# A gated delta-rule block with a routed feed-forward: the first block's solve moved into PSUM, and the head's copies, constants and loads reordered

## The reference

```python
q, k, v = x @ Wq.T, x @ Wk.T, x @ Wv.T;  gate = x @ Wg.T;  beta = sigmoid(x @ Wb.T)
alpha = exp(-exp(A_log) * softplus(x @ Wa.T + dt_bias))
q = q / norm(q) / sqrt(8);  k = k / norm(k)
def step(S, inp):                       # S: 8 x 8 for each sequence and head
    S = S * a_t
    delta = (v_t - k_t @ S) * beta_t
    S = S + outer(k_t, delta)
    return S, q_t @ S
ctx = rmsnorm(ys) * silu(gate);  x = layernorm(x + ctx @ Wo.T + bo)
# then a router picks one of 8 experts for each token: silu(x @ g.T) * (x @ u.T) @ d.T
# x = layernorm(x + that)
```

## Time and profile before

| | us |
|---|---|
| median of 3 runs | 792.31 (787.78 to 793.07) |
| the profiled execution, time | 794.0 |
| the profiled execution, span | 792.2 |
| busy: TensorE, VectorE, GpSimd, ScalarE | 682.4, 617.4, 654.0, 416.0 |
| first chunk of the recurrence starts | 39.5 |

### The profile page before, as it was taken

The page is one execution under the profiler, slowest core; times in us unless marked ns, Lnnn a source line. Parts: engine busy times, 40 slices in busy tenths (PEclk is TensorE's granted clock), DMA queues, the critical chain, the costliest instruction groups (busy, mean ns, idle before and its releaser), DMA issues.

```text
span 792.2 us, 13701 instructions
## 1 busy us (share of the span) xinstructions
PE 682.4 (86%) x3545; PEld 512.9 (65%) x3545; DVE 617.4 (78%) x1553; ACT 416.0 (53%) x1282; POOL 654.0 (83%) x799
## 2 busy tenths in 40 slices
PE   8577889999899998999989899697688869999990
PEld 3344546657576575755657566475577869999990
DVE  2699999999999999999999999999972533334340
ACT  4725454565655556564575645424224346666660
POOL 1669899989999999999999999999755765766664
PEclk9779999999999999999999999889859999999995
DMA  5922343323344233334333333204544556766730
GB/s 131 221 69 57 86 113 111 84 81 88 95 113 120 85 86 97 106 103 109 84 99 82 103 107 84 84 4 155 204 156 130 202 187 204 248 230 231 242 107 11
DMA packets 135917, 97.27 MB, mean 123 GB/s; under 512 B 95630, under 2 KB 110225, under 8 KB 135714
## 3 DMA queue, kind: packets, MB, share of 16 engines
q1 hardware_dynamic: 130514, 87.55, 37.5%
q0 software_dynamic: 4320, 8.43, 3.3%
q10 hardware_dynamic: 1008, 0.43, 0.2%
HBM read 39.80 MB, written 31.43 MB: 90 GB/s over the span
## 4 chain that ended last, share of the span: by engine, by line
DVE 36%; PE 34%; POOL 16%; issue 5%; ACT 3%; SPq 2%; DMA 1%; POOLq 0%; DVEq 0%; ACTq 0%
PE banks L432 10%; PE banks L654 8%; DVE banks L1811 6%; DVE upd L1799 6%; PE banks L445 5%; DVE banks L1785 5%; DVE prod L1769 4%; POOL q_prod L1257 4%; DVE banks L1795 4%; DVE mix L1789 3%; DVE upd L1780 3%; POOL u L1257 2%; PE banks L639 2%; PE banks L707 2%; POOL kkqk L1257 1%
## 5 line engine op out<-in xcount | busy, mean ns | idle before, releaser
L1257 POOL TENSOR_TENSOR q_prod<-s_keep,q_gam 128x512 f32<-128x512 f32 x128 | 139.9, 1096 | 17.4 <-ACT s_keep L964 16.2
L707 PE MATMUL banks<-q_prod,ident 128*128 128x256 f32 x496 | 119.1, 395 | 21.1 <-POOL q_prod L1257 21.1
L964 ACT ACTIVATE s_keep<-banks 128x128 f32<-128x128 f32 x128 | 49.7, 389 | 164.8 <-DVE upd L1799 164.8
L707 PEld LDWEIGHTS banks<-q_prod,ident 128*128 128x128 f32 x496 | 95.8, 198 | 45.8 <-POOL q_prod L1257 32.1
L542 DVE TENSOR_TENSOR hid<-banks,silu 128x384 f32<-128x384 f32 x71 | 39.6, 558 | 96.1 <-PE banks L432 85.5
L432 PE MATMUL banks<-xs_t,w_tile 128*128 128x128 f32 x852 | 108.9, 279 | 3.7 <-ACT silu L473 3.7
L1811 DVE TENSOR_REDUCE banks<-upd 128x128 f32<-128x640 f32 x127 | 105.1, 828 | 7.2
L654 PE MATMUL banks<-kkqk,ident 128*128 128x320 f32 (+2 forms) x272 | 91.5, 502 | 20.6 <-POOL kkqk L1257 8.1
L432 PEld LDWEIGHTS banks<-xs_t,w_tile 128*128 128x128 f32 x852 | 102.4, 195 | 4.6 <-issue 4.5
L1785 DVE TENSOR_REDUCE banks<-prod 128x64 f32<-128x576 f32 x128 | 93.7, 732 | 0.0
L654 PEld LDWEIGHTS banks<-kkqk,ident 128*128 128x128 f32 x272 | 60.0, 234 | 47.8 <-issue 20.7
(11 more groups left out here) (214 smaller groups left out, 1448.8 us busy)
## 6 DMA issues: line engine op xcount, KB each, us to landing
w_tile<-gate_up_we SPq DMA_DIRECT2D x71, 352.0 KB
xs<-x_sorted SPq DMA_DIRECT2D x71, 64.5 KB, 2.2
x_ct<-in_x_ct SPq DMA_DIRECT2D x16, 256.0 KB, 3.0
k_dram<-kq_s SPq DMA_DIRECT2D x16, 256.0 KB, 2.9
q_dram<-kq_s SPq DMA_DIRECT2D x16, 256.0 KB, 3.6
out<-v_s SPq DMA_DIRECT2D x16, 256.0 KB, 2.6
k_h<-k_dram SPq DMA_DIRECT2D x16, 256.0 KB, 3.1
out<-beta SPq DMA_DIRECT2D x16, 256.0 KB, 2.6
```

The lines of the kernel that those rows point to most:

```text
L707: i = mm(out, ident[:, :], q_prod[m][:, :, d, :], start=(m == 0 and d == 0), stop=(d == DH - 1), skip_group_check=True)
L1257: b.step(label, win, lambda: tt(out, x, y, op))
```

## The change

Four things, all in the head but two waits:

- Constants: dt_bias and A_log have a semaphore of their own, `s_head`, and are issued behind x_ct of block 1; z of block 0 waits for six loads. ScalarE's exp of A_log moves behind kq_s(0).
- Projections: block 0 in the order q, b, g, v; block 1 in the order k, b, g, z, q, v. The copy v_s(0) moves from ScalarE to VectorE, in front of `fold_weights`; k_n(1) moves from VectorE to GpSimd, between k_gam(0) and k_end(0). On ScalarE kq_s(1) moves behind decay_of(0), and softplus(0) ahead of k_ln(1).
- The solve of block 0: kkd, u1, u2, u3 are written to PSUM (banks of `y_ps`, after silu(1)), u1 a second time to SBUF ("u1_s"), so that each product has one operand in PSUM and one in SBUF; u_tmp and solve stay in SBUF.
- The sync queue: b_store(0) ahead of k_load(0), the loads of block 0 ahead of z_store(1), x_load of windows 2 and 3 later, the latter last.

```diff
-        n_early, n_const = 16 * 8, 16 * (len(tiles) - 7 + 2)
+        n_early, n_const = 16 * 6, 16 * (len(tiles) - 7 + 2)
...
                 load(e, s_early, "w_a", "w_q", "w_v")
+                e.dma_start(x_ct[1][:, :], t["x_ct"][:, 1, :]).then_inc(s_xct[1], 16)
                 for tile, src in ((dt_h, t["dt_bias"]), (neg_a, t["A_log"])):
                     e.dma_start(tile[:, :], src.rearrange("(h o) -> h o", o=1).unsqueeze(0)
-                                .to_broadcast([NB // 2, H, 1])).then_inc(s_early, 16)
-                e.dma_start(x_ct[1][:, :], t["x_ct"][:, 1, :]).then_inc(s_xct[1], 16)
+                                .to_broadcast([NB // 2, H, 1])).then_inc(s_head, 16)
...
                 project("q", 0, q_at, 0)
-                project("v", 2, v_at, 0)
                 project("b", 4, b_at, 0)
                 project("g", 3, g_at, 0)
+                project("v", 2, v_at, 0)
                 b.wait_dma(s_xct[1], 1)
-                b.wait(act, "z_s", 0)
-                project_heads("z", z_at, 1)
                 b.wait(dve, "k_n", 0)
                 project("k", 1, k_at, 1)
-                b.wait(act, "kq_s", 0)
-                project("q", 0, q_at, 1)
                 b.wait(act, "tanh", 0)
                 project("b", 4, b_at, 1)
                 b.wait(act, "silu", 0)
                 project("g", 3, g_at, 1)
-                b.wait(act, "v_s", 0)
+                b.wait(act, "z_s", 0)
+                project_heads("z", z_at, 1)
+                b.wait(act, "kq_s", 0)
+                project("q", 0, q_at, 1)
+                b.wait(dve, "v_s", 0)
                 project("v", 2, v_at, 1)
...
                 b.wait(act, "k_ln", a - 1)
+                b.wait(act, "kq_s", a - 1)
                 project("b", 4, pre_ps[:, 0, :])
...
                 b.step("kq_s", 0, lambda: A(kq_s[:, 1, :], pb[6], ACT.Copy))
-                b.wait(pe, "v", 0)
-                b.step("v_s", 0, lambda: A(v_s[:, :], post_ps, ACT.Copy, scale=-1.0))
-                if not b.dry:
+                if not b.dry:
+                    b.eng.wait_ge(s_head, 32)
+                    A(neg_a[:, :], neg_a[:, :], ACT.Exp).then_inc(s_neg_a, 1)
                     nc.scalar.preload_act_table_set("silu_and_others")
...
-                b.wait(pool if a > 2 else dve, "k_n", a - 1)
+                b.wait(pool, "k_n", a - 1)
...
+                b.wait(act, "k_r", 1)
+                b.wait(act, "kq_s", 1)
+                mul("k_n", 1, kq_s[:, 0, :], kq_s[:, 0, :], k_sq[:, :])
                 mul("k_end", 0, k_end[0][:, :, :, :, :].rearrange("p c b d j -> p b d j c"),
...
+                b.wait(pe, "v", 0)
+                b.step("v_s", 0, lambda: v.tensor_scalar(v_s[:, :], post_ps, -1.0, None, ALU.mult))
                 if not b.dry:
                     fold_weights(b.eng)
...
+                b.wait(act, "silu", 1)
+                kkd_ps, u1_ps = y_ps[1][:, 0:96], y_ps[1][:, 96:480].rearrange("p (n j c) -> p n j c", j=3, c=NCH)
+                u2_ps = y_ps[0][:, 0:256].rearrange("p (n j c) -> p n j c", j=2, c=NCH)
+                u3_ps = y_ps[0][:, 256:384].rearrange("p (n j c) -> p n j c", j=1, c=NCH)
...
-                for d, u in ((1, u1), (2, u2), (3, u3)):
+                for label, d, u in (("u1", 1, u1_ps), ("u1_s", 1, u1), ("u2", 2, u2_ps), ("u3", 3, u3_ps)):
...
+                b.wait(dve, "u2", 0)
+                mul("u_far", u_tmp[:, :, 0, :], u2_ps[:, :, 1, :], u1[:, :, 0, :])
+                mul("solve1", sv[:, :, 4:16:5, :], u1_ps[:, :, :, :], bh[:, :, 0:3, :])
+                b.wait(dve, "u_far", 0)
                 b.wait(dve, "u3", 0)
-                mul("solve1", sv[:, :, 4:16:5, :], u1[:, :, :, :], bh[:, :, 0:3, :])
-                mul("u_far", u_tmp[:, :, 0, :], u2[:, :, 1, :], u1[:, :, 0, :])
-                b.wait(dve, "u_far", 0)
-                mul("u3_a", u3[:, :, 0, :], u3[:, :, 0, :], u_tmp[:, :, 0, :], ALU.subtract)
+                mul("u3_a", u3_ps[:, :, 0, :], u3_ps[:, :, 0, :], u_tmp[:, :, 0, :], ALU.subtract)
                 b.wait(dve, "u3_a", 0)
-                mul("u_near", u_tmp[:, :, :, :], u1[:, :, 1:3, :], u1[:, :, 0:2, :])
+                mul("u_near", u_tmp[:, :, :, :], u1_ps[:, :, 1:3, :], u1[:, :, 0:2, :])
...
-                v_store(0, act)
-                b.wait(pe, "g", 0)
-                x_load(2)
+                v_store(0, dve)
+                b_store(0)
                 k_load(0)
-                b_store(0)
-                z_store(1, dve)
                 q_load(0)
                 v_load(0)
                 b_load(0)
+                z_store(1, dve)
                 v_store(1, dve)
-                b.wait(pe, "g", 1)
-                x_load(3)
+                x_load(2)
+                z_load(1)
                 q_store(1)
-                k_store(1, dve)
-                z_load(1)
                 v_load(1)
+                b_store(1)
+                k_store(1, pool)
                 q_load(1)
-                b_store(1)
                 k_load(1)
                 b_load(1)
+                x_load(3)
```

More of the change, by code:

```diff
@@ L171, in block_kernel @@
         s_const, s_setup, s_neg_a = sem("s_const"), sem("s_setup"), sem("s_neg_a")
-        s_wk, s_early, s_zero = sem("s_wk"), sem("s_early"), sem("s_zero")
+        s_wk, s_early, s_zero, s_head = sem("s_wk"), sem("s_early"), sem("s_zero"), sem("s_head")
         s_xct = [sem(f"s_xct{n}") for n in range(2)]
@@ L1108, in start_up @@
                 b.step("silu", 1, lambda: A(gate[1][:, :], y_ps[1], ACT.Silu))
[L1109 to L1112, removed]
                 if not b.dry:
@@ L1117, in start_up @@
                     nc.scalar.mul(neg_a[:, :], neg_a[:, :], -1.0).then_inc(s_neg_a, 1)
+                softplus(0)
                 b.wait(pe, "nk", 1)
@@ L1121, in start_up @@
                 b.step("k_r", 1, lambda: A(k_sq[:, :], k_sq[:, :], ACT.Exp, scale=-0.5))
-                softplus(0)
                 if not b.dry:
@@ L1125, in start_up @@
                 decay_of(0)
+                b.wait(pe, "q", 1)
+                b.wait_dma(s_kst, 1)
+                b.wait_dma(s_qst, 1)
+                b.step("kq_s", 1, lambda: A(kq_s[:, :, :], pre_ps[:, 0:2, :], ACT.Copy))
                 b.wait(act, "tanh", 1)
@@ L1572, in start_up @@
                     at += 2 * size
-                b.wait(act, "k_r", 1)
-                b.step("k_n", 1, lambda: v.tensor_tensor(kq_s[:, 0, :], kq_s[:, 0, :], k_sq[:, :], ALU.mult))
                 b.wait(act, "alpha", 0)
@@ L1577, in start_up @@
                 b.wait(pe, "kk", 0)
+                b.wait(act, "silu", 1)
+                kkd_ps, u1_ps = y_ps[1][:, 0:96], y_ps[1][:, 96:480].rearrange("p (n j c) -> p n j c", j=3, c=NCH)
+                u2_ps = y_ps[0][:, 0:256].rearrange("p (n j c) -> p n j c", j=2, c=NCH)
+                u3_ps = y_ps[0][:, 256:384].rearrange("p (n j c) -> p n j c", j=1, c=NCH)
                 for d in range(1, C):
-                    mul(f"kkd{d}", lag(kkd, lag_at[d], d), lag(chain_ps[0][:, 256:352], lag_at[d], d),
+                    mul(f"kkd{d}", lag(kkd_ps, lag_at[d], d), lag(chain_ps[0][:, 256:352], lag_at[d], d),
@@ L1580, in start_up @@
                         (a_h[0][:, :, 1:4, :], decays[0][:, :, 4:7:2, :], decays[0][:, :, 5:6, :])[d - 1])
                 b.wait_dma(s_bld, 1)
-                for d, u in ((1, u1), (2, u2), (3, u3)):
+                for label, d, u in (("u1", 1, u1_ps), ("u1_s", 1, u1), ("u2", 2, u2_ps), ("u3", 3, u3_ps)):
                     size = (C - d) * NCH
                     b.wait(dve, f"kkd{d}", 0)
-                    mul(f"u{d}", u[:, :, :, :].rearrange("p (e b) j c -> p e b (j c)", b=2),
+                    mul(label, u[:, :, :, :].rearrange("p (e b) j c -> p e b (j c)", b=2),
@@ L1586, in start_up @@
                         bh[:, :, d:C, :].rearrange("p (e b) j c -> p e b (j c)", b=2),
-                        kkd[:, lag_at[d]:lag_at[d] + 2 * size].rearrange("p (b n) -> p b n", b=2).unsqueeze(1)
+                        kkd_ps[:, lag_at[d]:lag_at[d] + 2 * size].rearrange("p (b n) -> p b n", b=2).unsqueeze(1)
                         .to_broadcast([P, DH, 2, size]))
+                b.wait(dve, "u2", 0)
+                mul("u_far", u_tmp[:, :, 0, :], u2_ps[:, :, 1, :], u1[:, :, 0, :])
+                mul("solve1", sv[:, :, 4:16:5, :], u1_ps[:, :, :, :], bh[:, :, 0:3, :])
@@ L1596, in start_up @@
                 b.wait(dve, "u_near", 0)
-                mul("u2_a", u2[:, :, :, :], u2[:, :, :, :], u_tmp[:, :, :, :], ALU.subtract)
+                mul("u2_a", u2_ps[:, :, :, :], u2_ps[:, :, :, :], u_tmp[:, :, :, :], ALU.subtract)
                 b.wait(dve, "u2_a", 0)
-                mul("u_last", u_tmp[:, :, 0, :], u1[:, :, 2, :], u2[:, :, 0, :])
-                mul("solve2", sv[:, :, 8:16:5, :], u2[:, :, :, :], bh[:, :, 0:2, :])
+                mul("u_last", u_tmp[:, :, 0, :], u2_ps[:, :, 0, :], u1[:, :, 2, :])
@@ L1601, in start_up @@
```

(5 more changed lines are left out.)

2 lines of the change are left out of this document (removed).

## The result

| | before | after |
|---|---|---|
| median of the runs, us | 791.72 (787.78 to 793.07, 4 runs) | 780.23 (779.25 to 784.0, 4 runs) |
| ratio, 95% interval | | 0.9863 (0.9822 to 0.9905) |
| profiled execution, us | 794.0 | 779.52 |
| its span, us | 792.2 | 777.7 |
| first kkd / first prod, us | 27.94 / 39.52 | 21.57 / 26.81 |

The change takes 11.5 us by the medians. A second series of the same kernel on another chip gave 781.83 us against 790.99, a ratio of 0.9878 (0.9835 to 0.9921), or 9.2 us. The two profiles are further apart, 14.5 us, and the first thing to learn here is why.

A forecast was written before the change was run, and what follows sets the result against it. Bound: a serial VectorE chain over sixteen windows, moved whole by an earlier first chunk. 4.4 (kkd) + 6.7 (solve) - 0.7 (given back) = 10.4 us; from 794.0 to 783.6, less 1.7 to the median, 781.9 (777.5 to 788.6).

The forecast's parts named there:

- Term 1, the start of z: First block on TensorE: with six loads awaited, z follows k at 5.75 us, q starts at 9.43, 1.86 us earlier.
- Term 2, kkd: First chunk on VectorE: kkd at 23.5 us instead of 27.94, 4.4 us earlier, with ends 3.4 and 5.6.
- The early end: Head, TensorE's clock level risen by 9.4 us: k_load issued at 14.8, kkd at 22.35, 5.6 us earlier.
- The arm that decides: Head, between q and kkd: kk (written out, read back, products, lag sums) decides at 24.5 us, alpha's arm at 24.1.
- Term 3, the solve: VectorE from kkd to prod: 4.8 to 5.4 us instead of 11.58 with one operand in PSUM; 6.7 us saved.
- the low end: Solve on VectorE: sixteen instructions at undisturbed prices by width sum to 4.8 us from kkd to prod.
- Term 4, the give-back: First two windows: waits for GpSimd's shifted queue and TensorE's sums give back 0.7 us, ends 0 and 2.5.
- GpSimd as the bound: Recurrence windows: only GpSimd's shift of 4.5 us carries through, not VectorE's 11; time 787.8 us; chance 0.12.
- No relief from PSUM: Solve on VectorE: operations on PSUM as slow as before, leaving 4.4 - 0.7, time 788.6 us; chance 0.06.
- The slower case: Later windows: kkd waits 1.3 us for TensorE in all fifteen, 13.9 us more, time 795.8; chance 0.08, intermediate cases included.

The follow-up runs named there:

- held kernel: Kernel before with one wait added: GpSimd starts k_gam only when VectorE has ended the solve, whose terms stay in SBUF; 787.92 us in one run.
- the three repeats: Kernel before, unchanged, profiled three more times on a chip where it takes 830.17 us; kkd at 24.87, 26.69 and 26.70 us.

## Why the prediction was right, step by step

| step | predicted | profile after |
|---|---|---|
| z | 5.75 | 6.42 |
| q of the first block | 9.43 | 8.35 |
| TensorE at the upper level | by 9.4 to 13.85 | by 6.4 |
| k_load issued | 14.8 to 17.1 | 13.82 |
| kkd | 22.35 to 24.5, taken 23.5 | 21.57 |
| kkd to prod | 4.8 to 5.4 | 5.24 |
| prod | 28 to 30 | 26.81 |
| second window's prod, behind the first | 33.5 to 35 | 33.99 |
| saved, profile to profile | 10.4 (7.1 to 12.4) | 14.5 |
| time | 781.9 (777.5 to 788.6) | 780.23 |

**What was right** is the mechanism and its accounting: a serial chain of VectorE that starts earlier is over earlier by as much. The solve is the step that carries the result, and its price from rows of undisturbed instructions held: u1 was to be 0.547 and was 0.56, the 128x128 product 0.283 and 0.28. The Trainium skill (VectorE: DVE Perf Modes, Rules for kernel authors) leaves two ways for elementwise work on a matmul result, to accept the plain rate of a PSUM source or to copy it to SBUF first where many operations follow. Read as I read it, as a rule to copy out, it would have let the solve gain nothing; the kernel with the solve alone gained 5.9 us, so here the measurement decides against that way. The Trainium skill's other rule (SBUF — State Buffer, Who interferes with whom), that VectorE with two SBUF inputs and GpSimd shut each other out and with one don't, is borne out from both sides: by the 0.28 us beside a busy GpSimd in the kernel after and by the 0.28 us with SBUF operands beside an idle one in the held kernel.

**Term 1, the start of z**, was 0.67 us too early. I took the landing of six loads by analogy with ident, 2.9 us. The last of them, w_v, took 4.20, as the chain of waits of the kernel after shows, with x_ct of the second block, 256 KB, now issued right behind it. That x_ct is the cause isn't shown. In the kernel with the constants alone, which has the same order of loads, w_v took 3.2 and w_g 4.1 us, so which one is late changes and that one is late doesn't:

```profile
2.17 4.20 DMA w_proj<-in_w_v
...
6.42 1.04 PE banks L644 x2
```

**Term 2, kkd**, is the term that was mis-sized: 4.4 us taken, 6.4 found, outside my ends of 3.4 and 5.6. Both ends came from one wrong assumption, that the rise seen at 13.85 was a property of the kernel that closing the gap could only shift. It was one outcome of several. The early end still let z, the norm and what lies between them run at the lower level until 9.4; in the trace z itself was fast (1.04 us), the norm too, and q came 1.1 us ahead of my time in spite of z's lateness. The arm that decides was the one I named, kk, and the price of v_store and b_store ahead of k_load is there (13.14 for b_store, 13.82 for k_load), but all of it stands 1 us earlier than my early end, and so does kkd (0.8).

**Term 3, the solve**, was 6.7 us taken and 6.34 found. The 0.36 us are two small sizes: the three products with the scattered output solve took 0.85, 0.59 and 0.38 us (I had 0.547 for the first in the low end), and the products that read and write the same PSUM tile 0.35 where 0.283 was the price.

**Term 4, the give-back**, was 0.7 taken and 0.46 found (33.99 - 33.53), from another cause. I had put it down to TensorE's sums in the third chunk and the second window's kkd. VectorE waited for neither. It is the pause of 0.51 us. The first sums of queries, which I had ending at 37 to 39 at the lower level, started at 29.83, took 2.68 us where they had taken 4.61, and were done long before VectorE read them at 37.02. (The 6.4 us that I took for them reach to the end of the sums behind them, L657, which the earlier trace rows doesn't show.) GpSimd's queue moved further than I had it, z_sum ending at 29.55 and not at about 32, since its own products weren't held up any more; the cover was large enough.

**Why a kkd 1.9 us early didn't leave the time below the forecast by more.** The forecast started from the profiled execution of before, and was moved by 1.7 us to the median. But that execution's head was the latest of those that were profiled: the six with the old gap have kkd at 24.87 to 27.94, 26.3 in mean. From that mean the change takes 4.8 us (to 21.5), and with 6.3 for the solve and 0.5 given back it is 10.6 us, between the 11.5 and the 9.2 of the two series. So my 10.4 hit the medians partly by luck: kkd was sized too small, against a reference that was too late by about as much.

**The rivals.** GpSimd as the bound (787.8) fell by the solve alone: GpSimd moved 1.6 us and the time 5.9. No relief from PSUM (788.6) fell by the 0.28 us. The slower case (795.8) wanted a mean wait of more than 1.07 us over the fifteen windows; in all profiles of the study the wait in question sums to 3.9 to 7.2 us in four to ten windows, 4.2 in the kernel after, and changes between runs of one kernel by as much as between kernels (before 5.6, and 7.1, 3.9 and 5.0 in the three repeats). That is a spread of 3 us that no edit here has in hand, and it is why the profiled pair overstates the change once more, by 1.4 us.

What stays open: the cause of the pause, and when TensorE's level first rises in an execution. The profiles show that it rose within k in six of fourteen, that none of the gaps up to 0.8 us lost it and that all above 2 us did, not what sets the moment of the first rise.

## What to carry to other kernels

When two engines that work side by side both read only SBUF, look at the mean of the same shape with and without the neighbour: a factor of nearly five (1.354 against 0.283 us) says that they shut each other out, and one operand in PSUM ends it for both, without holding either. In the head of a kernel, take out idle gaps of TensorE even where they look shorter than what they cost, and don't read the time of a clock step from one profile: profile the kernel before several times, and make the sum against the mean of the stretch in question. A moved step is worth what the slower of the arms behind it gives; here the constants (1.2 us) and the order (2.0) added up because the constants moved both arms, kk and alpha, by the same 1.3 us, while the order moved alpha's arm alone, until kk decided.

## What the runs showed of the hardware

- TensorE's level in the first 14 us is settled anew in each execution. With gaps up to 0.8 us in front of z the upper level was there by 7.6 us in seven of seven profiles, with gaps of 1.4 us and more in three of seven. In three of the others the level reached during k was lost at z or right behind it, after 2.1 to 2.4 us of idling, and the granted clock then read 0.50 from 9.5 to 11.0 us; in the fourth the rise is at 13.85, with no fall recorded.
- The exclusion works in both directions: GpSimd's k_end took 1.58 us beside the solve in SBUF and 1.27 beside the one in PSUM, its four kkqk 3.94 and 3.33, its kk products of the second block 2.56 and 2.10.
- Of the early 64 KB loads one took 4.1 to 4.2 us to land (w_v in the kernel after, w_g in two others) with a 256 KB load issued right behind them, where ident, another 64 KB load, had taken 2.9 us in the kernel before. That one caused the other isn't shown.
- The table load on ScalarE behind silu of the second block took 1.28 us in the timeline, and the next instruction, the change of sign of exp(A_log), started at once (15.27 + 1.28 = 16.55, the instruction at 16.57).
- VectorE paused for 0.51 us with nothing to wait for that the profile shows, in five of five profiles of the fast solve in PSUM; in the one with twelve waits added earlier in the program, on another chip, the pause was gone.
- With a scattered output VectorE's products took 0.85, 0.59 and 0.38 us (384, 256 and 128 elements) in the kernel after, and 0.83, 0.58 and 0.38 with all operands in SBUF and GpSimd held, where plain ones took 0.547, 0.418 and 0.283.
